# Layer-1 mixer: query rows written by residue, both exponentials over adjacent columns, pair 0's tail behind pair 1's attention; layer ends split by image pair; fewer idle products

## What is computed

```python
out = conv2d(x, w1, b1) + conv2d(x, w3, b3, pad=1) + conv2d(x, w5, b5, pad=2)
...
c = out * ca
...
cbam_out = c * sa
q = conv2d(out, wq, bq).reshape(B, -1, N).transpose(0, 2, 1)
k = conv2d(out, wk, bk).reshape(B, -1, N).transpose(0, 2, 1)
v = conv2d(out, wv, bv).reshape(B, C, N)
...
dist_sq = q2[:, :, None] + k2[:, None, :] - 2.0 * jnp.einsum('bnc,bmc->bnm', q, k)
similarity = jnp.exp(-dist_sq / (2.0 * sigma * sigma))
attn = jax.nn.softmax(similarity, axis=-1)
ao = jnp.einsum('bnm,bcm->bnc', attn, v)
non_local = out + ao.reshape(B, C, H, W)
cat = jnp.concatenate([cbam_out, non_local], axis=1)
return conv2d(cat, tail_w, tail_b)
```

## Time and profile before

| | us |
|---|---|
| median of 3 runs | 191.16 (191.05 to 191.4) |
| profiled execution, its own time | 190.52 |
| its span, first to last instruction | 188.7 |

### The profile page before, as it was taken

How to read it: one execution, slowest core, us unless ns; L and a number is a source line. 1 busy time by engine, 2 the same in 40 slices (tenths; PEclk the granted TensorE clock), 3 DMA queues, 4 the chain that set the end, 5 groups by cost and what they waited for, 6 DMA issues and landing times.

```text
span 188.7 us, 3175 instructions
## 1 busy us (share of the span) xinstructions
PE 176.2 (93%) x1185; PEld 87.0 (46%) x1191; DVE 116.7 (62%) x312; ACT 123.9 (66%) x201; POOL 44.8 (24%) x62
## 2 busy tenths in 40 slices
PE   7999999999997999999999999999999996999991
PEld 2554324449786574322222355452224895353230
DVE  1476889758732744946545353586575798587565
ACT  2465997745438776765765650587775897588772
POOL 6162412000100102005973000020760022030660
PEclk9999999999999999999999999999999999999999
DMA  6999700000000000000000000000000000000001
GB/s 204 401 423 414 280 2 0 0 0 3 5 0 0 3 0 3 0 0 0 0 3 2 0 0 0 0 0 3 0 2 0 3 2 2 3 0 0 0 0 56
DMA packets 3088, 8.56 MB, mean 45 GB/s; under 512 B 521, under 2 KB 1041, under 8 KB 2945
## 3 DMA queue, kind: packets, MB, share of 16 engines
q1 hardware_dynamic: 2736, 7.73, 10.3%
q0 software_dynamic: 192, 0.50, 0.7%
q10 hardware_dynamic: 144, 0.13, 0.3%
HBM read 8.10 MB, written 0.26 MB: 44 GB/s over the span
## 4 chain that ended last, share of the span: by engine, by line
PE 67%; DVE 13%; ACT 8%; POOL 6%; issue 4%; POOLq 1%; ACTq 0%; DVEq 0%
PE bank L454 13%; PE banks L386 7%; PE banks L312 7%; PE banks L387 6%; POOL total L1620 6%; PE bank L325 5%; PE banks L650 4%; PE bank L317 4%; PE banks L369 3%; ACT hidden L893 2%; ACT rstd L861 2%; PE bank L434 1%; PE banks L625 1%; PE bank L397 1%; ACT sq_sim L979 1%
## 5 line engine op out<-in xcount | busy, mean ns | idle before, releaser
L893 ACT ACTIVATE hidden<-banks,pack_l 128x1024 f32<-128x1024 f32 x40 | 44.5, 1112 | 17.3 <-PE banks L387 16.6
L454 PE MATMUL bank<-hidden,w 128*64 128x512 f32 (+1 forms) x144 | 37.1, 593 | 0.7 <-ACT hidden L893 0.7
L386 PE MATMUL banks<-split_x,w_hi 128*128 128x512 f16 x64 | 24.6, 384 | 0.0
L387 PE MATMUL banks<-split_x,w_lo 128*128 128x512 f16 x64 | 24.3, 379 | 0.0
L312 PE MATMUL banks<-idle_work 128*128 128x512 bf16 x66 | 18.4, 408 | 1.5 <-DVE idle_work L1199 1.2
L1620 POOL TENSOR_TENSOR total<-total,term 128x512 f32<-128x512 f32 x12 | 17.1, 1422 | 1.9 <-DVE term L1176 1.3
L1597 POOL CAST split_x<-normed 64x256 f16<-64x256 f32 x12 | 6.1, 505 | 45.8 <-DVE normed L1081 42.1
L386 PEld LDWEIGHTS banks<-split_x,w_hi 128*128 128x128 f16 x64 | 6.2, 97 | 22.4 <-issue 13.4
L857 ACT ACTIVATE squares<-bank 128x256 f32<-128x256 f32 x18 | 6.9, 383 | 14.3 <-PE bank L317 12.8
L454 PEld LDWEIGHTS bank<-hidden,w 128*64 128x64 f32 x144 | 7.2, 134 | 14.1 <-issue 12.5
L1176 DVE TENSOR_TENSOR term<-relu_sim,bank 128x512 f32<-128x512 f32 x12 | 7.8, 684 | 7.8 <-PE bank L397 5.3
(11 more groups left out here) (320 smaller groups left out, 325.3 us busy)
## 6 DMA issues: line engine op xcount, KB each, us to landing
w_stage<-in_w SPq DMA_DIRECT2D x3, 512.0 KB, 12.7
w_stage<-in_w SPq DMA_DIRECT2D x1, 1024.0 KB, 9.2
conv<-in_conv SPq DMA_DIRECT2D x1, 800.0 KB, 7.3
w<-in_w SPq DMA_DIRECT2D x3, 256.0 KB, 12.9
w<-in_w SPq DMA_DIRECT2D x1, 512.0 KB, 9.9
toeplitz<-in_toeplitz SPq DMA_DIRECT2D x1, 512.0 KB, 10.5
gauss<-in_gauss SPq DMA_DIRECT2D x1, 512.0 KB, 12.0
pack_l<-in_pack_l SPq DMA_DIRECT2D x1, 469.0 KB, 11.3
```

The lines of the kernel that those rows point to most:

```text
L386: mm(out, w1_hi[l][:, at:at + 128], split_x[h][:, :], start=True, stop=False)
L387: last = mm(out, w1_lo[l][:, at:at + 128], split_x[h][:, :], start=False, stop=True)
L454: last = mm(out[64 * h:64 * h + 64, cut], w2[l][:, (f * NE + e) * CH:(f * NE + e + 1) * CH], hidden[v % 3][:, h * 512 + cut.start:h * 512 ...
L893: act(hidden[u % 3][:, :], both[u % 2][:, :], ACT.Gelu, bias=P(f"l{l}", "e_b1")[:, e * fc + f:e * fc + f + 1]).then_inc(S["moe_gelu"], 1)
```

## The change

- PE starts with 7 idle products, not 11; after norm 5 stand 3, not 4.
- The query rows are written by residue (position r*64+c from column 4c+r) by the instructions that make them; the softmax exp reads and writes adjacent columns. ACT squares both halves' queries, the second behind the channel gate's tanh; POOL's square is gone.
- Layer 1's mixer, PE: `gated_tokens(1)` ahead of the last quarter of `attend(0)`; `tail_attended(0)` behind `attend(1)`; both centres of norm 4 behind both tails. DVE: `token_features(1)`, `value_rows(1)` ahead of `normalise(0)`, `add_input(0)` behind `normalise(1)`. Norm 4 is as all others, without idle products.
- Layers 1 to 3 end by pair: DVE adds term 6 to pair 0's rest and POOL to pair 1's; DVE makes both last terms; POOL makes pair 0's x, DVE pair 1's. PE and SP wait for POOL where they need pair 0.

```diff
-                sp.wait_ge(S["x_ready"], 2 * 8 + j + 1 - 2)
+                if j:
+                    sp.wait_ge(S["x_ready"], 2 * 8 + j + 1 - 2)
+                else:
+                    sp.wait_ge(S["end_pool"], 6)
                 sp.dma_start(a["out"][:, j * PIX:(j + 1) * PIX], chunk(x[8], j)).then_inc(S["out_stored"], 16)
...
+        def quads(ap):
+
+            return ap.rearrange("p (c r) -> p c r", r=4)
+
+        def by_residue(ap):
+
+            return ap.rearrange("p (r c) -> p c r", r=4)
...
+        BY_POOL = {4: 2, 6: 4, 8: 6}
...
-        NORM_TAIL = [5, 2, 4, 4, 0, 4, 2, 4, 1]
+        NORM_TAIL = [5, 2, 4, 4, 0, 3, 2, 4, 1]
...
-        def variance_ps(k, j):
-
-            return bank[6][:, j * PIX:(j + 1) * PIX] if k == 4 else bank[6 + j][:, 0:PIX]
...
-                if k == 4 and j:
-                    pe.wait_ge(S["ln_rstd"], 2 * k + 1)
-                mm(variance_ps(k, j), P("first", "average"), chunk(squares, j), start=True, stop=True)\
+                mm(bank[6 + j][:, 0:PIX], P("first", "average"), chunk(squares, j), start=True, stop=True)\
...
-                return lambda j: pe.wait_ge(S["x_ready"], x_count(k, j))
+                def ready(j):
+                    if j == 0 and k in BY_POOL:
+                        pe.wait_ge(S["end_pool"], BY_POOL[k])
+                    else:
+                        pe.wait_ge(S["x_ready"], x_count(k, j))
+                return ready
...
-                    if l != 1:
-                        pe.wait_ge(S["ln_rstd"], 2 * k + 2)
+                    pe.wait_ge(S["ln_rstd"], 2 * k + 2)
...
-                        if l == 1:
-                            average(k, 1)
                         router((0, 1))
-                        if l == 1:
-                            up_straight(1, 0)
                         up_straight(0, 1)
                         router((2, 3))
                     elif u == 1:
-                        if l != 1:
-                            up_straight(1, 0)
+                        up_straight(1, 0)
...
-            busy(11, bank[0][:, :])
+            busy(7, bank[0][:, :])
...
-                pe.wait_ge(S["qk_sq"], j + 1)
-                pe.wait_ge(S["qk_sq_pool"], j + 1)
+                pe.wait_ge(S["qk_sq"], 2 * j + 2)
...
+            gated_tokens(1)
             attend(0, range(3, 4))
-            gated_tokens(1)
             values(1)
-            tail_attended(0)
             spatial_gates(1)
             attend(1)
-            center(4, 0, x[3], x_ready(3))
+            tail_attended(0)
             tail_gated(1)
             tail_attended(1)
+            center(4, 0, x[3], x_ready(3))
+            center(4, 1, x[3], x_ready(3))
             average(4, 0)
-            center(4, 1, x[3], x_ready(3))
+            average(4, 1)
+            busy(NORM_TAIL[4], bank[0][:, :])
             experts(1, 4)
...
-                pe.wait_ge(S["x_ready"], x_count(4, j))
+                x_ready(4)(j)
...
-            def cast_first(k):
+            def split(k, l):
+
                 sc.wait_ge(S["ln_out"], 2 * k + 1)
                 act(chunk(split_x[0], 0)[0:64, :], chunk(normed[k], 0)[0:64, :], ACT.Copy).then_inc(S["split_act"], 1)
-
-            def split(k, l):
-
-                cast_first(k)
                 nc.scalar.preload_act_table_set("gelu_and_others")
...
-                    act(attn[:, cut].rearrange("p (m r c) -> p m r c", m=2, r=4),
-                        simil[:, cut].rearrange("p (m c r) -> p m r c", m=2, r=4), ACT.Exp,
-                        bias=P("first", "minus_one")).then_inc(S["attn"], 1)
+                    act(attn[:, cut], simil[:, cut], ACT.Exp, bias=P("first", "minus_one")).then_inc(S["attn"], 1)
...
-                act(chunk(query_rows, j)[0:32, :], chunk(QK, j)[0:32, :], ACT.Square).then_inc(S["qk_sq"], 1)
-                sc.wait_ge(S["ca_s"], j + 1)
-                tanh_half(ca[:, 2 * j:2 * j + 1], gate_ps[j][:, 0:1]).then_inc(S["ca_e"], 1)
+                for h in range(HALVES):
+                    r = slice(64 * h, 64 * h + 32)
+                    act(by_residue(chunk(query_rows, j)[r, :]), quads(chunk(QK, j)[r, :]), ACT.Square)\
+                        .then_inc(S["qk_sq"], 1)
+                    if h == 0:
+                        sc.wait_ge(S["ca_s"], j + 1)
+                        tanh_half(ca[:, 2 * j:2 * j + 1], gate_ps[j][:, 0:1]).then_inc(S["ca_e"], 1)
                 similarities(j)
                 gate_pixels(j)
             nc.scalar.preload_act_table_set(ROOTS)
-            square(4, 0)
-            inverse_deviation(4, 0)
-            square(4, 1)
-            cast_first(4)
-            inverse_deviation(4, 1)
-            nc.scalar.preload_act_table_set("gelu_and_others")
+            norm(4)
+            split(4, 1)
...
-                summed = st.mark(TT(rest[:, :], rest[:, :], total[:, :], ALU.add))
+                TT(rest[:, :], rest[:, :], total[:, :], ALU.add).then_inc(S["end_vector"], 1)
                 ve.wait_ge(S["moe_y"], base - fc_of[l])
                 ve.wait_ge(st.sem, copied)
                 STT(term6[:, :], bank[4 + (NE - 2) % 2][:, :], P(f"l{l}", "e_b2")[:, NE - 2:NE - 1], wide6,
                     ALU.add, ALU.mult).then_inc(S["moe_term"], 1)
-                ve.wait_ge(st.sem, summed)
+                ve.wait_ge(S["end_vector"], 4 * l - 3)
                 ve.wait_ge(S["moe_term"], terms)
-                st.mark(TT(rest[:, :], rest[:, :], term6[:, :], ALU.add))
+                TT(chunk(rest, 0), chunk(rest, 0), chunk(term6, 0), ALU.add).then_inc(S["end_vector"], 1)
                 ve.wait_ge(S["last_wide"], l)
                 for j in range(INNER):
                     if j == 0:
                         ve.wait_ge(S["moe_y_first"], l)
                     else:
                         ve.wait_ge(S["moe_y"], base)
-                    st.link(STT(chunk(term[1], j), chunk(last_y[j], j), P(f"l{l}", "e_b2")[:, NE - 1:NE],
-                                chunk(last_wide, j), ALU.add, ALU.mult))
-                    TT(chunk(x[2 * l + 2], j), chunk(term[1], j), chunk(rest, j), ALU.add).then_inc(S["x_ready"], 1)
+                    STT(chunk(term[1], j), chunk(last_y[j], j), P(f"l{l}", "e_b2")[:, NE - 1:NE], chunk(last_wide, j),
+                        ALU.add, ALU.mult).then_inc(S["end_vector"], 1)
+                ve.wait_ge(S["end_vector"], 4 * l)
+                ve.wait_ge(S["end_pool"], 2 * l - 1)
+                TT(chunk(x[2 * l + 2], 1), chunk(term[1], 1), chunk(rest, 1), ALU.add).then_inc(S["x_ready"], 2)
...
-                    V.tensor_copy(chunk(query_rows, j)[64 * h + 32:64 * h + 64, :], chunk(QK, j)[64 * h:64 * h + 32, :])\
-                        .then_inc(S["qk_lin"], 1)
+                    V.tensor_copy(by_residue(chunk(query_rows, j)[64 * h + 32:64 * h + 64, :]),
+                                  quads(chunk(QK, j)[64 * h:64 * h + 32, :])).then_inc(S["qk_lin"], 1)
...
-            normalise(0)
             token_features(1)
             value_rows(1)
-            add_input(0)
+            normalise(0)
             gate_both(1)
             normalise(1)
+            add_input(0)
             add_input(1)
             norm(4)
...
-            for j in range(INNER):
-                po.wait_ge(S["qk_sb"], j + 1)
-                G.tensor_tensor(chunk(query_rows, j)[64:96, :], chunk(QK, j)[64:96, :], chunk(QK, j)[64:96, :], ALU.mult)\
-                    .then_inc(S["qk_sq_pool"], 1)
+            def last_sums(l):
+
+                po.wait_ge(S["end_vector"], 4 * l - 3)
+                po.wait_ge(S["moe_term"], (NE - 1) * l)
+                G.tensor_tensor(chunk(rest, 1), chunk(rest, 1), chunk(term[(NE - 2) % 3], 1), ALU.add)\
+                    .then_inc(S["end_pool"], 1)
+                po.wait_ge(S["end_vector"], 4 * l - 1)
+                G.tensor_tensor(chunk(x[2 * l + 2], 0), chunk(term[1], 0), chunk(rest, 0), ALU.add)\
+                    .then_inc(S["end_pool"], 1)
+
             split(4, 1)
             accumulate(1, (corner_parts, corners_01, corners_23, gated_recall))
+            last_sums(1)
             split(6, 2)
             accumulate(2)
+            last_sums(2)
             g64 = lambda t: t.rearrange("p (g c) -> p g c", c=64)
             po.wait_ge(S["q_max"], 1)
@@ -1645,6 +1657,7 @@
                 .then_inc(S["q_sb"], 1)
             split(8, 3)
             accumulate(3)
+            last_sums(3)
```

More of the change, by code:

```diff
@@ L116, in metaformer @@
             c_tok ca_e ca_h ca_in ca_r ca_s ca_top cbam_done conv_done conv_loaded
-            conv_out conv_split corner_w ctx_ps ctx_sb dist dve_chain e_key e_lev0 e_lev e_tok_ps field_bias final_ps
+            conv_out conv_split corner_w ctx_ps ctx_sb dist dve_chain e_key e_lev0 e_lev e_tok_ps end_pool end_vector field_bias final_ps
             first_loaded gated_c gauss_loaded idle_work_zero k_bias k_len k_ps k_sq key_peak l0_exp l0_exp_in l0_first l0_base l0_b2s l0_loaded l0_mixed
@@ L122, in metaformer @@
```

(4 more changed lines are left out.)

## The result

The changed kernel has a median of 188.22 us (187.9 to 188.74, 4 executions), the kernel before on the same chip, in turn with it, 191.28: a ratio of 0.985 with a 95% interval of 0.9822 to 0.9877, or 2.4 to 3.4 us less. The forecast was 188.1. The two profiled executions differ by less, 190.52 and 188.44, spans 188.7 and 186.6 us. Why they differ by 2.1 and the medians by 3.1 is the main thing the experiments had to settle. For the profiled execution by itself the forecast was 187.5, and it took 188.44.

A forecast was written before the change was run, and what follows sets the result against it. No engine alone bounds the kernel, but one chain that changes engines (67% PE). Terms 0.75 + 1.6 + 0.25 + 0.25 + 0.2 = 3.05 take the profiled 190.52 to 187.5; the median, 0.64 above, to 188.1; range 187.0 to 189.6.

The forecast's parts named there:

- Start, 0.75: Kernel start: with 7 idle products, not 11, the first centre product starts near 4.4 us, 0.75 earlier.
- The step that put the centre product at the landing of `pack_first`: Start: data lands at 3.8 and 4.0; with 0.2 for semaphore and 0.2 for weight load, centre product near 4.4.
- The step that took the clock to rise near 4.4: Start: PE's clock goes from 1.2 to 2.4 GHz near 4.4 us, after 3.2 us of products without a gap.
- the prediction's own sign of being wrong: Start: the forecast is wrong if, among other signs, the low clock lasts past 5.5 us.
- start does not move: Rival, chance 0.12: transfers land later, or the clock goes up late as products end before it rises; time 188.85.
- Pair 0's exps, 0.97: Mixer: pair 0's two exps save 1.2 us, but pair 1's convolution on PE then ends last, so 0.97 gained.
- Query rows, 0.5 given back: Mixer: stepped writes cost 0.30 per 256 columns; with ACT's second square, distances(1) give back 0.5 of the 0.97.
- Attention of pair 1, 1.5: Mixer: exps and spatial gates of pair 1 end earlier, so attention(1) starts at 66.27, 1.5 before 67.76.
- Norm 4, a gain of 0.1: End of layer 1's mixer: in the common order, the table load before the first gelu starts at 72.6, not 74.20.
- Ends, 0.25, 0.25, 0.2: Ends of layers 3, 2 and 1: splitting sums by pair between DVE and POOL gains 0.25, 0.25 and 0.2 us.
- the step that SP's first issue is not in the way: Layer 3's end: SP issues pair 0's store first, 0.35 an issue, without delaying the second, issued at 186.35.

The follow-up runs named there:

- e5: Kernel before with 7 idle products at its start in place of 11, nothing else: median 190.21 us, ratio to before 0.9931.
- e1: Changed kernel with 11 idle products at the start again in place of 7: median 189.10 us, ratio to before 0.9904.
- e3: Changed kernel with adjacent query rows, POOL's second square and the exp reading by residue again, order as changed: median 189.89 us, ratio to before 0.9939.
- e4: Changed kernel with layer 1's mixer in the old order on PE and DVE, residue and norm 4 as changed: 189.08 us, ratio to before 0.989.
- e7: Changed kernel with only pair 1's rest on POOL at the layer ends, DVE making both x: median 188.65 us, ratio to before 0.9843.
- e12: Changed kernel with 3 idle products at the start in place of 7: median 190.21 us, ratio to before 0.9947.
- e10: Changed kernel with the keys' squares on POOL and ACT's two query squares ahead of the channel gate's tanh: 188.04 us, ratio to before 0.9834.

## Why the prediction was right, and where it was not

The total was right, 188.1 against 188.22, and in part by luck: terms that missed did so in both directions. In the profiles the sum is 0.24 + 1.33 + 0 + 0.27 + 0.20 = 2.04 where 3.05 was forecast, and the profiled execution took 188.44 where 187.5 was. The median came out because in medians the start is worth 1.3, more than its term, by about what the mixer and the ends lack.

- **Start, 0.75.** The step that put the centre product at the landing of `pack_first` was right (4.27 for 4.4), with two errors that cancel: the landing came 3.5 us after the issue for the 3.3 of the earlier trace rows, and the product started 0.05 after it, where 0.4 was put for semaphore and weight load and no run shows that. The step that took the clock to rise near 4.4 as in the profile of before was wrong: it is not the same moment in each execution, and in nine of the ten profiles with seven products part or all of the centre product is at 1.2 GHz. By the prediction's own sign of being wrong, a low clock past 5.5 us, it failed here: in the changed kernel's profile the clock rose near 5.6. The term as a difference of the two profiles is 0.24; as a difference of medians it is 1.3 (1.0 to 1.7, e5) or 1.0 (e1). That this is so because before's medians hold late starts as well is argued, from e1's profile; the rival "start does not move", which named the clock as a reason, is refuted by e5's medians, not by the two profiles.
- **Pair 0's exps, 0.97.** Right: attention of pair 0 starts 0.97 + 0.24 + 0.16 earlier, bound by the convolution. The 0.16 was not in the sum: with POOL's square gone DVE is through sooner and PE waits less for pair 0's channel gate. Before, DVE's product of one column ran beside POOL's square; after, it runs alone:

```profile
50.35 0.31 DVE L1356 TENSOR_TENSOR ca_in<-ca_relu 8x1 f32<-8x1 f32 x1
```

```profile
50.12 0.15 DVE L1360 TENSOR_TENSOR ca_in<-ca_relu 8x1 f32<-8x1 f32 x1
```

- **Query rows, 0.5 given back.** Right in size, 1.37 at the attention against 0.89 at the distances, and in the place: PE waited for ACT's second square. The writes cost 636 - 398 = 238 ns for 256 columns where 300 was taken, on DVE 379 a copy where 700 was: the 0.91 for two that the prediction started from had POOL's square beside it, which the change takes away (alone the adjacent copy took 283).
- **Attention of pair 1, 1.5.** 1.87 - 0.24 = 1.63 measured. Gates and exps end together, as the working had it (65.72 and 65.74). The exps' price was mis-sized: over adjacent columns they take 728 ns and not the 631 of L1047, so pair 1's two end 1.0 sooner after their start and not 1.2 (2.34 and 1.34 in the timelines).
- **Norm 4, a gain of 0.1.** Wrong sign: from attention to first down product it is 8.99 us before and 9.29 after. The table load came even sooner than forecast (72.21 + 0.24 = 72.45 for 72.6), but the step looked at ACT's table load and not at what PE had in front of the first down product. By the timelines the old order had a first straight product done before pair 1's average and another while pair 1 was still being normalised; now all stand in one line on PE behind pair 0's norm, until 75.18. The 9.29 comes again in e3 and 9.27 in e4; no run undoes norm 4's order alone, so the cause is read from the timelines. That makes the mixer 1.57 - 0.24 = 1.33 in place of 1.6.
- **Ends, 0.25, 0.25, 0.2.** Layers 3 and 2 gave 0.20 and 0.27, the sharing of SBUF between POOL and DVE included: 0.97 for a sum that was put at 0.6 behind a wait, 0.72 and 0.67 for the two x. At layer 3 the step that SP's first issue is not in the way was wrong: pair 1's x is 2.27 earlier than before (186.59 and 184.32), 0.42 of it from this end, and the span keeps 0.20, as e7 explains. Layer 1 gave 0: the centre product waits for the idle products behind the layer either way, and behind norm 5 PE now waits for its input. Pair 1's half is normalised at 110.66 + 0.85 = 111.51, which is where the second L725 product starts (111.52 in the trace); four idle products of 0.22 each would have ended before it, at 111.25. No run puts the fourth one back.

```profile
110.66 0.85 DVE L1430 TENSOR_TENSOR normed<-bank,rstd 128x256 f32<-128x256 f32 x2 [2.19 <-ACT rstd L868]
```


The Trainium skill's rule on 16-byte lines (SBUF — State Buffer, Door 1: The DMA port swizzle) is borne out for the reads, 1224 to 728 ns, and now for ACT's writes, at about the reads' price: 238 / 256 = 0.93 ns more a column against (1224 - 728) / 512 = 0.97. The Trainium skill's rule on shared interfaces (GPSIMD Engine Reference, Key points), that POOL contends with DVE instructions of two SBUF inputs, is borne out by e7: x alone 0.42, beside POOL's 0.67.

## What to carry to other kernels

Where two branches end together, undo each part alone before judging it: here order alone gave nothing and residue alone left 0.6 on the table, and together they gave 1.6. Compare profiles by a span less the moment at which a variable start is over; a profile is one draw of it: here the kernel before was drawn twice near its best. When idle products are cut at a start, find out by a run how few still bring the clock up: seven did better than eleven by 1.0 to 1.3 us and better than three by 2.0. A first store that comes late can hold the last one: look at the issuing engine's queue too.

## What the runs showed of the hardware that was not expected

- PE's clock rises at the start at different moments for the same work in front of it: near 4.4 us in two profiles of before, near 5.3 in e1's, and in kernels with seven idle products anywhere that makes the centre product 1.13 to 2.07 us long. With three (e12) it was still low at 7.73, where five idle products took 2.06 us for 1.24. The granted clock of the profiles reads 1.00 over the low stretches all the same, so the clock at the start is read from the products' own spacing.
- ACT writing 32 x 256 fp32 with a step of 256 bytes takes 636 ns against 398 adjacent. DVE's copy of the same form takes 379 ns alone, where the adjacent one took 283 alone and 590 beside POOL. Beside POOL the stepped one is as slow, 596 (e10).
- A POOL sum of 128 x 256 took 0.72 us at the ends, and 0.97 when it started with a DVE sum of 0.43 beside it, which itself is not slowed.
- SP takes 0.35 us to issue a store, 0.43 when it follows directly on another, and the second starts 0.04 after the first is through (184.41 and 184.45).
